# A four-layer graph network on one core: no barrier between the attention's output and the third layer, and that layer's second tile loaded in three pieces

## What is computed

```
h = relu(layernorm(x)); x = x + gin(h, src, dst)                 # layer "l0"
h = relu(layernorm(x)); x = x + edge_attention(h, src, dst, ...) # the attention
h = relu(layernorm(x)); x = x + sage(h, src, dst)                # "l2", the third layer
h = relu(layernorm(x)); x = x + linear(segment_sum(w * h[src], dst)) # "l3"
# sage: agg = segment_sum(h[src], dst); h @ w_self.T + b_self + (agg / deg) @ w_neigh.T + b_neigh
# attention, at its end: y = h + (sums_v / sums) @ Wo + bo; layernorm(y) * gamma + beta
```

## Time and profile before

| | us |
|---|---|
| median of 3 runs | 5554.05 |
| lowest and highest run | 5548.2, 5557.44 |
| the profiled execution's own time | 5533.22 |
| its span in the trace | 5531.4 |
| TensorE busy in the span | 4526.3 |
| VectorE busy | 3188.8 |

### The profile page before, as it was taken

How to read it: one execution, slowest core, us unless ns; L and a number is a source line. 1 busy time by engine, 2 the same in 40 slices (tenths; PEclk the granted TensorE clock), 3 DMA queues, 4 the chain that set the end, 5 groups by cost and what they waited for, 6 DMA issues and landing times. The chain is left out here.

```text
span 5531.4 us, 87976 instructions
## 1 busy us (share of the span) xinstructions
PE 4526.3 (82%) x25332; PEld 3174.1 (57%) x25333; DVE 3188.8 (58%) x4531; ACT 1789.2 (32%) x3407; POOL 2014.9 (36%) x1926
## 2 busy tenths in 40 slices
PE   6888665565899968888888888888884399999999
PEld 4656332222788844554555455555553388888888
DVE  6323988877211058889998989898985710000000
ACT  2433267889200030112333344455552400001000
POOL 0320026300000007777777777777774400000000
PEclk9989999988999999999999999999995599999999
DMA  8885467755766643445555556666665366669998
GB/s 185 171 155 132 112 220 274 289 232 253 305 279 273 273 144 84 116 135 141 158 159 162 173 179 179 195 200 193 199 205 166 135 280 279 279 255 296 300 293 264
DMA packets 736267, 1150.51 MB, mean 208 GB/s; under 512 B 310041, under 2 KB 659421, under 8 KB 717343
## 3 DMA queue, kind: packets, MB, share of 16 engines
q1 hardware_dynamic: 461057, 653.45, 34.7%
q10 hardware_dynamic: 211504, 349.71, 18.0%
q0 software_dynamic: 63600, 146.16, 10.7%
HBM read 762.49 MB, written 393.26 MB: 209 GB/s over the span
## 5 line engine op out<-in xcount | busy, mean ns | idle before, releaser
L1505 POOL DMA_INDIRECT at_qg<-q_d,at_slot x1616 | 1655.7, 1025 | 496.1 <-issue 492.4
L713 PE MATMUL bw_ps<-bw_mov,bw_sta 128*128 128x392 bf16 x7056 | 1575.2, 346 | 22.2 <-issue 8.3
L1548 PE MATMUL at_psk<-at_kp,at_hot 128*128 x4848 | 613.7, 233 | 338.3 <-DVE at_qg L1626 287.0
L713 PEld LDWEIGHTS bw_ps<-bw_mov,bw_sta 128*128 128x128 bf16 x7056 | 630.9, 101 | 372.2 <-issue 103.8
L1548 PEld LDWEIGHTS at_psk<-at_kp,at_hot 128*128 128x128 bf16 x4848 | 435.6, 100 | 684.9 <-issue 477.9
L713 PE MATMUL ba_ps<-ba_mov,ba_sta 128*128 128x392 bf16 x2352 | 513.8, 365 | 317.9 <-ACT ba_ps L672 136.3
L676 DVE TENSOR_TENSOR ba_mov<-iota,key 128x3136 bf16<-128x3136 f16 x294 | 526.8, 1792 | 132.2 <-PE ba_ps L713 127.0
L713 PEld LDWEIGHTS ba_ps<-ba_mov,ba_sta 128*128 128x128 bf16 x2352 | 242.1, 103 | 589.7 <-issue 475.2
L697 DVE TENSOR_TENSOR bw_sta<-bw_raw,kw 128x1024 bf16<-128x1024 bf16 x882 | 557.5, 688 | 0.0
L1054 PE MATMUL l2agg<-tiles,h 128*128 128x256 f32 (+1 forms) x2450 | 525.0, 376 | 22.4 <-PEq L1075 22.4
L1054 PE MATMUL l3agg<-tiles,h 128*128 128x256 f32 (+1 forms) x2450 | 525.8, 377 | 5.2 <-ACT h L915 5.2
(11 more groups left out here) (412 smaller groups left out, 3811.8 us busy)
## 6 DMA issues: line engine op xcount, KB each, us to landing
adj_d<-ba_stage ACTq DMA_DIRECT2D x49, 3136.0 KB, 9.1
l0adjt<-adj_d SPq DMA_DIRECT2D x23, 6272.0 KB, 17.2
tiles<-adj_d SPq DMA_DIRECT2D x23, 6272.0 KB, 17.3
tiles<-adw_d SPq DMA_DIRECT2D x23, 6272.0 KB, 20.4
adw_d<-xall ACTq DMA_DIRECT2D x65, 1568.0 KB
adw_d<-bw_stage ACTq DMA_DIRECT2D x33, 1568.0 KB
at_rel<-rel_d SPq DMA_DIRECT2D x101, 512.0 KB
at_qg<-q_d,at_slot POOLq DMA_INDIRECT x1616
```

Source lines behind the costliest of these rows:

```text
L713: ins = pe.matmul(self.ps[:, bass.DynSlice(place, WCOL)], self.sta[:, k, u // 2, :, u % 2], self.mov[:, u // 2, :, u % 2], start=False, st ...
L1505: pool.indirect_dma_start(out=qg[:, ring, b, :], out_offset=None, in_=q_d[:, :], in_offset=bass.IndirectOffsetOnAxis(ap=slot[:, ring, b:b ...
L1548: ins = pe.matmul(ps_k[:, at:at + KW], hot[:, par, sum(ROUNDS[:r]) + u, :], kp[:].rearrange("p j k n -> p (j k n)")[:, bass.DynSlice(place ...
```

## The change

`attention_output` no longer ends in a barrier. Its SBUF and PSUM buffers are now allocated in the context of the layers that follow (`c.after`), so that nothing reuses their places, and the small buffers and PSUM banks of the two later layers are put in a `Space` that both share: its aggregate banks are the two of `ps_t[1]`, its mid banks those of `ps_t[0]`, its out banks those of `ps_p[1]`. The third layer's second tile, whose place holds v and h, is loaded in three pieces: blocks 0 to 27 once four batches have been added to x, 28 to 41 after six, 42 to 48 after seven. Each piece raises `s_tile[1]` by 16, so the waits of the odd groups count 32 more.

```diff
+class Space:
+    def __init__(self, sb):
+        self.aggT, self.midT, self.own = sb("aggT", [P, 2, 2 * P]), sb("midT", [P, 2, 2 * P]), sb("own", [P, 2, 2, D])
@@ aggregate_layer(..., space=None, freed=None)
-        aggT = sb("aggT", [P, 2, 2 * P])
-        midT = sb("midT", [P, 2, 2 * P])
-        ps_agg = [psum(f"agg{k}", [P, 512]) for k in range(2)]
-        ps_mid = [psum(f"mid{k}", [P, 512]) for k in range(2)]
-        ps_out = [psum(f"out{k}", [P, 512]) for k in range(2)]
+        if space is None:
+            space = Space(sb)
+            space.agg, space.mid, space.out = ([psum(f"{n}{k}", [P, 512]) for k in range(2)] for n in ("agg", "mid", "out"))
+        aggT, midT, own, ps_agg, ps_mid, ps_out = space.aggT, space.midT, space.own, space.agg, space.mid, space.out
...
-        own = sb("own", [P, 2, 2, D])
...
+        freed_by = [(0, 28, 4), (28, 42, 6), (42, NB, 7)]
...
-                pe.wait_ge(s_tile[par], 16 * turn + 16 * par)
+                pe.wait_ge(s_tile[par], 16 * turn + par * (16 + late))
...
-        load(1, 1, 0)
+        late = 0
+        if freed:
+            for lo, hi, n in freed_by:
+                freed(sp, n)
+                sp.dma_start(tiles[:, 1 ^ flip, :].rearrange("p (a n) -> p a n", n=NPAD)[:, :, lo * P:hi * P], adj[2:4, :, lo * P:hi * P].rearrange("a p n -> p a n")).then_inc(s_tile[1], 16)
+            late = 16 * (len(freed_by) - 1)
+        else:
+            load(1, 1, 0)
@@ AttentionOutput.run
-        with ExitStack() as ctx:
-            attention_output(self.nc, self.c, self, ctx)
+        attention_output(self.nc, self.c, self, self.c.after)
@@ attention_output, at its end
-    nc.all_engine_barrier()
+    space = c.space = Space(sb)
+    space.agg, space.mid, space.out = ([b[:, k * 512:(k + 1) * 512] for k in range(2)] for b in (ps_t[1], ps_t[0], ps_p[1]))
+    c.rows_used = lambda eng, batches: q["x_summed"].wait(eng, batches)
@@ layers
-        aggregate_layer(nc, c, h, c.adj_d, "l2", w, SageEpilogue, ..., following="n3", then=...)
-        aggregate_layer(nc, c, h, c.adw_d, "l3", w3, LinearEpilogue, ..., flip=1, out=out)
+        aggregate_layer(nc, c, h, c.adj_d, "l2", w, SageEpilogue, ..., following="n3", space=c.space, freed=c.rows_used, then=...)
+        aggregate_layer(nc, c, h, c.adw_d, "l3", w3, LinearEpilogue, ..., flip=1, out=out, space=c.space)
```

More of the change, by code:

```diff
@@ L1001, in load_first, with aggregate_layer @@
             nc.sync.dma_start(tile.rearrange("p (a n) -> p a n", n=NPAD)[:, :, lo * P:hi * P], adj[0:2, :, lo * P:hi * P].rearrange("a p n -> p a n")).then_inc(q, 16)
-def aggregate_layer(nc, c, h, adj, name, weights, epilogue, tiles=None, following=None, ready=False, rows=None, flip=0, then=None, gated=False, out=None):
+class Space:
+    def __init__(self, sb):
+        self.aggT, self.midT, self.own = sb("aggT", [P, 2, 2 * P]), sb("midT", [P, 2, 2 * P]), sb("own", [P, 2, 2, D])
+def aggregate_layer(nc, c, h, adj, name, weights, epilogue, tiles=None, following=None, ready=False, rows=None, flip=0, then=None, gated=False, out=None, space=None, freed=None):
     ve, pe, act, sp = nc.vector, nc.tensor, nc.scalar, nc.sync
@@ L2244, in layers @@
         h, w, w3, tiles = attention_layer(nc, c, a, following)
-        aggregate_layer(nc, c, h, c.adj_d, "l2", w, SageEpilogue, tiles=tiles, ready=True, rows=c.norm.s_rows, following="n3", then=lambda tile: load_first(nc, c, tile, c.adw_d, True))
-        aggregate_layer(nc, c, h, c.adw_d, "l3", w3, LinearEpilogue, tiles=tiles, ready=True, flip=1, out=out)
+        aggregate_layer(nc, c, h, c.adj_d, "l2", w, SageEpilogue, tiles=tiles, ready=True, rows=c.norm.s_rows, following="n3", space=c.space, freed=c.rows_used, then=lambda tile: load_first(nc, c, tile, c.adw_d, True))
+        aggregate_layer(nc, c, h, c.adw_d, "l3", w3, LinearEpilogue, tiles=tiles, ready=True, flip=1, out=out, space=c.space)
 def place_first_weights(c, sb):
```

## The result

| | before | after |
|---|---|---|
| median of 6 runs, us | 5544.44 | 5522.07 |
| lowest and highest run, us | 5537.16, 5557.44 | 5517.18, 5528.5 |
| profiled execution, us | 5533.22 | 5525.06 |
| its span, us | 5531.4 | 5523.1 |

The ratio is 0.9952 with a 95% interval of 0.9939 to 0.9965: the change is faster by half a percent, by 26.6 us of 5544.44 (19.4 to 33.8) by the ratio and by 22.4 by the medians. The three runs of before that the prediction knew (median 5554.05) were the slower half of the six; the other three lie at 5537.16 to 5540.68.

A forecast was written before the change was run, and what follows sets the result against it. TensorE was taken as the bound, idle 22.40 us at the barrier before the third layer. Ending the first aggregate at 4423.5 instead of 4446.3 saves 22.8 us: 5554.05 - 22.8 = 5531.3 us, range 5522 to 5543.

The forecast's parts named there:

- the sum: Whole forecast: the first aggregate ends at 4423.5 instead of 4446.3, 22.8 us less, taking the median 5554.05 to 5531.3 us.
- this case: Main case, chance 0.86: without the barrier TensorE starts the third layer early, gaining 22.8 us; 5523 to 5537 with scatter.
- step 1: Hand-over to the third layer: without the barrier TensorE starts 1.09 us after its last product, at 4401.04.
- the time before 4396 moved: Sign of being wrong: the part of the program ahead of the last attention product, at 4396, shifts.
- Step 2: Third layer's first aggregate: 21.3 us plus 1.2 us for a start at the lower clock, ending at 4423.5.
- Step 3: First aggregate's wait for rows of h2: no pause in the stream, only a floor, ending no earlier than 4421.4.
- Step 4: Second tile's three pieces take 11.7, 7.1 and 4.8 us; the last lands at 4422.2, 1.3 us before it is needed.
- Step 5: After the first aggregate: copies and bias additions finish almost 10 us before the epilogue; later groups keep their 23.0 us period.
- B: Whole first aggregate at the lower clock, 42.6 us: gain only 2.7 us, 5551.4 us; chance 0.04.
- C: Low clock lasting into the second aggregate too, another 21.3 us lost: slower, 5572.7 us; chance 0.03.
- D: Last tile piece takes 18.6 us, so the second aggregate waits: gain 10.2 us, 5543.8 us; chance 0.04.
- E: Something else holds TensorE until the last row of h2: gain 1.4 us, 5552.7 us; chance 0.03.

The follow-up runs named there:

- e0: The changed kernel with the same added register operations as eb_before: median 5672.06 us, ratio 1.0261 to the kernel before.
- e6: e0 with TensorE's first aggregate matmul of the third layer waiting for 29 rows of h2: 5674.5 us, ratio 1.0274 to the kernel before.
- e4: e0 with the second tile loaded in two pieces, 42 blocks after six batches and 7 after the seventh: 5678.76 us, ratio 1.0280.
- e3: e0 with the second tile loaded in one piece once all seven batches are added to x: 5691.05 us, ratio 1.0297.
- e7: e0 with the second tile loaded in seven pieces of 896 KB, each as its batch is added to x: 5676.77 us, one run.
- e8: The same program as e0 run once more, on another chip: 5681.86 us, one run.
- e5: e0 with TensorE's first aggregate matmul of the third layer waiting for 35 rows of h2: 5682.28 us, ratio 1.0283 to the kernel before.
- eb_before: The kernel before with a register operation added ahead of each wait on a count from a table; base of the series: 5696.21 us, ratio 1.0311.

## Why the prediction came out as it did

The mechanism was right in the main, and so was the gain; the time was forecast 9.2 us too high, and that comes from the level on which the gain was set. The measured 5522.07 us lie outside the 5523 to 5537 that the sum gave for this case, and barely inside the wider 5522 to 5543.

*The sum.* 22.8 us were predicted to the second aggregate. Measured: 23.6 (trace of the pair, to the third aggregate), 22.9 (trace of e0 against the base), 22.4 and 24.2 (medians).

*The step that failed* is the term in the Sum from which the gain is subtracted: the gain is carried over to a median of 5554.05 with a scatter of -5.9 and +3.4 around it, as the paragraph ahead of step 1 announces. Six runs gave 5544.44, 9.6 us less, and the later sessions 5526.03, 5525.29 and 5529.52 (one run). The medians of one unchanged kernel thus lie up to 29 us apart, more than the whole gain; how much of that is the chip and how much the session was not separated. Set on 5544.44, the same sum gives 5521.6 against 5522.07 measured. That the three runs it knew were the high ones was bad luck, but three runs were too narrow a measure of the scatter, and the prediction had a hint in its hand: it noted that the profiled execution was 20.8 us under the median and drew nothing from it for the range. One of its own signs of being wrong was met as well: the time before 4396 moved, by 15.7 us. That was scatter in the stage of the edge scores, whose place the trace shows and whose cause it does not: over the ten kernels of the series the last product's start moves by 17.6 us, but the one with the earliest start (e6) does not have the shortest waits for gathers (87.6 us from 1400 to 4320, against 68.1 in e4).

*Step 1* (a start 1.09 us behind the last product) was too dear by just that: the first matmul stands at 4415.36, within the modelled end of the last product. The six semaphore increments and first waits cost nothing behind a running matmul. The 1.09 us were there because TensorE's queue stood at the barrier; which part of them was the way out of the barrier and which the increments behind it was not separated.

*Step 2* (0 to 5 us at the lower level, 1.2 us taken) held: it cost nothing in the changed kernel's profile, 1.2 us in e0, in e3 (22.47 us for 98 records) and in e4 (22.49), 1.3 in e7, 1.1 in e8.

*Step 3* said that there is no pause, only a floor. With a start 1.1 us earlier than in step 1 and at the upper level TensorE did run into the floor, and so into a pause: 0.75 us at block 42. The floor was right within 0.7 us: it let the aggregate end 0.45 us behind the last row, and the copy came 1.15 us behind it.

*Step 4* met the pieces: 11.7, 7.1 and 4.8 us against 11.8, 6.8 and 4.8 (in e0 and e8 the second took 8.1 and 8.2 us, which nothing waited for). It called the last piece what is late next if the aggregate ends at its earliest, and that is the 0.31 us seen. The Trainium skill ("DMA: Bandwidth & Descriptors", "Anatomy of one DMA — SWDGE (gpsimd) path") gives about 2.0 us plus bytes over 436 GB/s for a DMA that GpSimd issues; these come from SyncE. Carried over to them it makes an estimated 10.4 and 4.1 us for the first and the last; the trace shows 11.8 and 4.8. Whatever is constant in a piece's time lies beside other work and does not add up, as e7 shows.

*Step 5* held: the copies and additions ended at about 4450.4 and 4450.2 (the second addition is 4443.42 for 6.77 us), ahead of the first epilogue at 4459.25, and the third aggregate to the fourth is still 23.0 us.

*The rivals.* B and C (clock low through the first aggregate) did not occur in any of the eleven traces of the change and of the series; the largest loss was 2.6 us. The Trainium skill ("TensorE: Matmul & The Clock Gate", "HAM oscillation — how this bites in real kernels") tells of a kernel whose waits for loads inside a matmul stream bring the half rate back each time. The traces agree for the pauses of 6.7, 7.0 and 12.5 us (e4, e5, e3), in which the granted clock fell from 1.00 to 0.50, and not for those of 0.31 and 0.75 us. D (the last piece slow) did not occur with three pieces, but e4 shows that its mechanism is real: the same 896 KB took 11.4 us behind a large piece. E fell: idle before the first aggregate is gone.

## What to carry to other kernels

Here the barrier cost what the engine that sets the end could have done behind it, and the gain needed that engine's early start. The transfers must still be made to arrive in time, here in pieces of which the last is small and issued when no other is under way; with one piece 14.9 of the 22.9 us turned into a wait with a cold start behind it. When the gain is a few tenths of a percent, read it in the stretch of the change: forecast a difference, and widen the range of the time by how far the unchanged kernel itself moves between sessions, which three runs do not show.

## What was not expected of the hardware

The register operation added before each wait on a table's count made the programs 170 us longer. In the first building stage TensorE's group of one matmul per count, before and then in eb_before:

```profile
L713 PE MATMUL ba_ps<-ba_mov,ba_sta 128*128 128x392 bf16 x2352 | 513.8, 365 | 317.9 <-ACT ba_ps L672 136.3 <-issue 112.3 <-DVE ba_sta L676 68.6
```

```profile
L713 PE MATMUL ba_ps<-ba_mov,ba_sta 128*128 128x392 bf16 x2352 | 678.2, 396 | 333.3 <-issue 171.6 <-ACT ba_ps L672 134.1 <-DVE ba_sta L676 25.0
```

Busy time rises by 164.4 us over 2352 counts, 70 ns for each, of which the mean duration of a matmul shows 31 ns (365 to 396). The operations were added on ScalarE too, but there they do not bind: its copies of this stage (L737) waited 221.4 us for TensorE's matmuls before and 405.1 in eb_before. In the second stage, with three matmuls for each of as many counts, it rises by 9.3 us only (1575.2 to 1584.5). So the operation is hidden behind three matmuls and not behind one. What in it takes the 70 ns was not tried.

The start at the lower clock after a pause of TensorE cost 1.6 to 2.6 us in eight cases with pauses of 4.7 to 22.4 us, in no order with the pause; it is about half of the time that the stream ran at the lower level, 3.3 to 5.4 us by the granted clock. Where the stream went on from the last product without a pause it cost 0 to 1.3 us. Whether the last product, of the same 3.36 us each time, itself ends at the upper level differs from run to run of the same work: it did in the profiles of before, the changed kernel and e5 and not in the other nine.
